# A convolution stage of eight image pairs: the work between two pairs is placed inside the steps of the next pair

## The reference, cut to what matters

```
x = x + L0(groupnorm(x))      # L0: minus the L1 distance between 3x3 patches and 128 filters
                              #     -sum over channel, tap of |W - patch|
out = act_quant(bn(conv3x3(x, wq1)))          # wq1, wq2: 4-bit weights, 7 of 9 taps kept
x = act_quant(bn(conv3x3(out, wq2)) + x)      # clip to 0..1, round to 15 levels
# then two layers on 784 tokens per image: additive attention, mixture of experts,
# linear attention, spectral filter; the change doesn't touch them
```

## Time and profile before

| | |
|---|---|
| median of 3 runs | 13612.95 us (13599.4 to 13621.69) |
| the profiled execution | 13581.18 us, span 13579.4 us |
| mean granted TensorE clock | 0.977 of full speed |
| PE busy | 12646.4 us, 93% |
| DVE busy | 11715.2 us, 86% |
| ACT busy | 11095.8 us, 82% |

### The profile page before, as it was taken

One profiled execution on the slowest core, in us unless ns is written; L12 is line 12 of the kernel. 1 busy time (PEld: TensorE's weight loads), 2 busy tenths in 40 slices (PEclk: granted clock), 3 DMA queues, 4 the chain that ended last, 5 costly groups with the idle time before them and its releaser, 6 DMA issues. The chain is left out here.

```text
span 13579.4 us, 320458 instructions
## 1 busy us (share of the span) xinstructions
PE 12646.4 (93%) x128658; PEld 6147.6 (45%) x128658; DVE 11715.2 (86%) x21048; ACT 11095.8 (82%) x7140; POOL 254.3 (2%) x125
## 2 busy tenths in 40 slices
PE   8999999999999999999867999999999999999999
PEld 3433433333333333333323455555555555555556
DVE  8888888888988888888799988998888998888981
ACT  7878778787887878878688888888888888888882
POOL 0000000000000000000000000000000000000000
PEclk9999999999999999999989999999999999999999
DMA  0000000000000000000010111111111111111113
GB/s 11 2 6 2 4 4 2 6 2 6 2 2 6 2 6 2 2 6 2 14 48 2 40 48 50 48 51 44 46 47 50 49 49 46 45 49 50 46 51 104
DMA packets 290098, 356.95 MB, mean 26 GB/s; under 512 B 28040, under 2 KB 242960, under 8 KB 288656
## 3 DMA queue, kind: packets, MB, share of 16 engines
q1 hardware_dynamic: 288656, 335.48, 8.4%
HBM read 314.14 MB, written 21.23 MB: 25 GB/s over the span
## 5 line engine op out<-in xcount | busy, mean ns | idle before, releaser
L139 PE MATMUL c_acc<-c_ring,c_onehot 128*32 128x392 f32 x73728 | 6128.9, 495 | 235.3 <-DVE c_ring L260 145.0
L260 DVE TENSOR_SCALAR c_ring<-c_xn,c_w 128x1568 f32 x5760 | 5642.3, 1048 | 648.9 <-PE c_acc L139 642.8
L186 ACT ACTIVATE c_ring<-c_xn,c_w_neg 128x1568 f32 x3456 | 5331.2, 1606 | 980.5 <-PE c_acc L139 962.6
L887 ACT ACTIVATE t_ring<-t_ring 128x3136 f32<-128x3136 f32 (+4 forms) x2160 | 5138.8, 2403 | 552.2 <-DVE t_ring L1189 536.5
L1189 DVE TENSOR_SCALAR t_ring<-t_proj 128x784 f32<-128x784 f32 (+4 forms) x10240 | 4276.1, 489 | 564.3 <-PE t_psS L798 551.0
L139 PEld LDWEIGHTS c_acc<-c_ring,c_onehot 128*32 128x32 f32 x73728 | 2472.5, 111 | 3891.7 <-issue 3746.9
L798 PE MATMUL t_psS<-t_ring,t_vhot 128*32 128x392 f32 (+3 forms) x36864 | 2834.0, 436 | 189.4 <-ACT t_ring L887 159.1
L755 PE MATMUL t_psC<-t_filter_work 128*128 128x392 f32 (+3 forms) x6144 | 1645.3, 402 | 47.5 <-ACT t_filter_work L874 47.5
L798 PEld LDWEIGHTS t_psS<-t_ring,t_vhot 128*32 128x32 f32 x36864 | 1027.1, 111 | 1248.5 <-issue 555.4
L755 PEld LDWEIGHTS t_psC<-t_filter_work 128*128 128x128 f32 x6144 | 1135.2, 192 | 710.3 <-ACT t_filter_work L874 65.6
L766 PE MATMUL t_psS<-t_filter_work 128*128 128x98 f32 (+2 forms) x4096 | 956.2, 356 | 0.0
(11 more groups left out here) (212 smaller groups left out, 3375.6 us busy)
## 6 DMA issues: line engine op xcount, KB each, us to landing
t_filter_work<-in_toep_dram SPq DMA_DIRECT2D x256, 393.0 KB, 3.3
t_filter_work<-mix_scratch SPq DMA_DIRECT2D x512, 192.0 KB, 2.4
t_filter_work<-in_toep_dram SPq DMA_DIRECT2D x256, 197.0 KB, 2.6
t_filter_work<-mix_scratch SPq DMA_DIRECT2D x512, 64.0 KB, 1.8
mix_scratch<-t_filter_work SPq DMA_DIRECT2D x4, 2048.0 KB, 9.5
c_xin<-in_x_dram SPq DMA_DIRECT2D x8, 784.0 KB, 4.3
x_scratch<-c_xout SPq DMA_DIRECT2D x8, 784.0 KB, 3.4
t_proj<-x_scratch SPq DMA_DIRECT2D x16, 392.0 KB, 3.2
```

What stands on the lines that cost most here:

```text
L139: mm = pe.matmul(acc[32 * g:32 * g + 32, ch, 0:HALF], onehot[:, 31 - r:63 - r], ring[:, r % RING, g, ch * HALF:(ch + 1) * HALF], start=Fal ...
L186: act.activation(ring[:, r % RING, g, :].rearrange("c (i h w) -> c i h w", i=2, h=HW), xn[:, :, bass.ds(dy, HW), bass.ds(dx, HW)], ACT.Rel ...
L260: dve.tensor_scalar(ring[:, r % RING, g, :].rearrange("c (i h w) -> c i h w", i=2, h=HW), xn[:, :, bass.ds(dy, HW), bass.ds(dx, HW)], w0[: ...
L887: act.activation(ring[:, st % RINGS, 0:n], ring[:, st % RINGS, 0:n], ACT.Tanh).then_inc(th.s, 1)
```

## The change: what it does

- The loops over the taps are gone. All 288 steps are written out, in one body per pair; pairs 0 and 7 have a body of their own, and pairs 1 to 6 run as three turns of a loop over two bodies (`pairs`). xin and xn get two buffers, used in turn; x1 gets a tensor of its own (x1p), and the convolutions write to three PSUM banks of their own (pst).
- Each engine walks through the steps of pair p and, after fixed step numbers, issues pieces of other work (`tracks`): the x1 of pair p-1 (after step 2), its convolutions (steps 7 to 41), the norm of pair p+1 (steps 60 to 112), the pair's own box sums (steps 130 to 150).
- The box sums move from POOL to DVE. Their PE part is inside the steps. The zero matmuls that opened acc go; step 0 opens it with start=True. Two operations per pair are new on DVE: xin less the weights' sum (s_xs). x1 is then one operation per bank that reads acc, where it was three for all.
- Which engine makes a tile is set by a running sum of costs (`distance_steps`), in which EXTRA_VEC stands for DVE's other work. MERGED is 0, so the "merged" form never occurs and every tap keeps a tile.
- At step 0 PE waits, bank by bank, until DVE has read acc. The token stage is as before.

```diff
-VEC_SHARE = [3 if r % 2 == 0 else 2 for r in range(32)]
-VEC_TILES = sum(VEC_SHARE); ACT_TILES = 4 * 32 - VEC_TILES
+MERGED = 0; TAP_A, TAP_B = 0, 1
...
+COST = dict(vec=0.95, act=1.55, merge=1.85)
...
+    out = []
...
+    for s in range(steps):
+        if s in EXTRA_VEC: vec += EXTRA_VEC[s]
...
+                e = "vec" if vec + COST["vec"] <= act + COST["act"] else "act"
+                if e == "vec": vec += COST["vec"]
+                else: act += COST["act"]
...
+        out.append(step)
...
+AT_X1 = 2
+AT_C1 = [7, 11, 15, 19]
+AT_A1 = [c + 6 for c in AT_C1]
+AT_Q = [c + 8 for c in AT_C1]
+AT_C2 = [22, 24, 30, 32]
+AT_OUT = [c + 5 for c in AT_C2]
...
+AT_GN = dict(stats=60, aggr=65, mean=72, dev=78, devs=86, var=92, std=96, xn=104, shift=110)
...
+AT_BOX = [130, 134, 138, 142]; AT_BOX_SUM = 150
+EXTRA_VEC = {AT_X1: 2.6, **{s: 0.8 for s in AT_Q}, **{s + 2: 2.2 for s in AT_OUT}, 62: 2.5, 66: 0.5, 80: 0.6, 93: 0.5, 106: 1.4, 111: 1.1, **{s: 1.9 for s in AT_BOX}}
+DISTANCE = distance_steps()
...
+            one_pair(0, 0, True, False)
+            with e.Fori(0, (NP - 2) // 2) as pp:
+                one_pair(2 * pp + 1, 1, False, False, pp)
+                one_pair(2 * pp + 2, 0, False, False, pp)
+            one_pair(NP - 1, 1, False, True)
...
+        def in_step(step, due, tracks):
+            for n, track in enumerate(tracks):
+                while due[n] is not None and due[n] <= step:
+                    due[n] = next(track, None)
+        def run(tracks, body):
+            due = [next(track, None) for track in tracks]
+            body(lambda step: in_step(step, due, tracks))
+            in_step(999, due, tracks)
...
+                sp.dma_start(x1[bass.ds(p, 1)].rearrange("a i c t -> c (a i) t"), tmp[:, :, :].rearrange("c (i h) t -> c i (h t)", i=2)).then_inc(s_st, 16)
...
+                    wait(sp, s_x1, 4 * p)
+                    wait(sp, s_x, 16 * p + 16)
+                    sp.dma_start(xin2[:, 1 - buf], ai["x"][bass.ds(p + 1, 1)].rearrange("a i c t -> c (a i) t")).then_inc(s_x, 16)
+                if not first: store(p - 1)
...
-            with pool.Fori(0, NP) as p:
-                pool.wait_ge(s_xn, 2 * p + 2)
...
-                link(pool.tensor_tensor(rows3[:, :, :, :], xn[:, :, :, 0:HW], xn[:, :, :, 1:1 + HW], ALU.add), 1)
-                link(pool.tensor_tensor(rows3[:, :, :, :], rows3[:, :, :, :], xn[:, :, :, 2:2 + HW], ALU.add), 2)
...
-                link(pool.tensor_tensor(box[:, :, :, :], rows3[:, :, 0:HW, :], rows3[:, :, 1:1 + HW, :], ALU.add), 3)
-                pool.tensor_tensor(box[:, :, :, :], box[:, :, :, :], rows3[:, :, 2:2 + HW, :], ALU.add).then_inc(s_box, 1)
...
+            def normalize(q):
+                yield AT_GN["mean"]
+                wait(pe, s_stat, 2 * q + 2)
                 pe.matmul(psg[:, 0:4], group_avg[:, :], mv[:, :, :], start=True, stop=True).then_inc(s_gmean, 1)
-                pe.wait_ge(s_dev, p + 1)
+                yield AT_GN["devs"]
+                wait(pe, s_dev, q + 1)
                 pe.matmul(psg[:, 8:10], group_avg[:, :], dev2[:, :], start=True, stop=True).then_inc(s_gdev, 1)
...
+            def tail(d):
+                for c in range(4):
+                    yield AT_C1[c]
+                    if c == 0:
+                        wait(pe, s_x1, 4 * d + 4)
+                        wait(pe, s_accr, 4 * d)
+                    if c == 3: wait(pe, s_a1, 4 * d + 1)
+                    conv(pst[:, c % 3, 0:HALF], wq1, x1p, c // 2, c % 2, s_c1)
+                for c in range(4):
+                    yield AT_C2[c]
+                    if c % 2 == 0: wait(pe, s_q, 4 * d + c + 2)
+                    if c < 3: wait(pe, s_a1, 4 * d + c + 2)
+                    else: wait(pe, s_accr, 4 * d + 1)
+                    conv(pst[:, (c + 1) % 3, 0:HALF], wq2b, xq, c // 2, c % 2, s_c2)
+            def box_sum(p):
+                yield AT_BOX_SUM
+                wait(pe, s_box, p + 1)
...
+                    pe.matmul(acc[:, ch, 0:HALF], minus_half[:, :], box[:, ch // 2, ROWS * (ch % 2):ROWS * (ch % 2 + 1), :].rearrange("c h w -> c (h w)"), start=False, stop=False, skip_group_check=True)
...
-                    pe.matmul(acc[:, ch, 0:HALF], zero_bf[:, 0:128], zero_bf[:, 128:128 + HALF], start=True, stop=False, skip_group_check=True)
...
+                def body(done):
+                    for s, step in enumerate(DISTANCE):
+                        wait(pe, s_tv, VEC_UP[-1] * p + VEC_UP[s])
+                        wait(pe, s_ta, ACT_UP[-1] * p + ACT_UP[s])
+                        for ch in range(4):
+                            if s == 0 and not first: wait(pe, s_x1, 4 * (p - 1) + ch + 1)
+                            for g in range(4):
+                                r = step[g][2]
+                                mm = pe.matmul(acc[32 * g:32 * g + 32, ch, 0:HALF], onehot[:, 31 - r:63 - r], ring[:, s % RING, g, ch * HALF:(ch + 1) * HALF],
+                                               start=(s == 0), stop=(s == NSTEP - 1), skip_group_check=True)
+                            if s == NSTEP - 1 and ch < 3: mm.then_inc(s_acc, 1)
+                        mm.then_inc(s_free, 1)
...
+                yield AT_GN["std"]
+                wait(act, s_gvar, q + 1)
                 act.activation(gstd[:, :], gvar[:, :], ACT.Sqrt).then_inc(s_gstd, 1)
...
+            def tail(d):
                 for c in range(4):
...
+                    yield AT_A1[c]
+                    wait(act, s_c1, 4 * d + c + 1)
+                    act.activation(act1[:, c, :], pst[:, c % 3, 0:HALF], ACT.Relu, scale=bn_q[:, 0:1], bias=bn_shift[:, 0:1]).then_inc(s_a1, 1)
...
-                    dve.tensor_scalar(xn[:, im, 1:1 + HW, 1:1 + HW], xin[:, im, :].rearrange("c (h w) -> c h w", h=HW), gmv[:, im, 0:1], grstd[:, im:im + 1], ALU.subtract, ALU.mult).then_inc(s_xn, 1)
-                dve.wait_ge(s_xn, 2 * p + 2)
-                n[0] += 1; dve.memset(pad[:, 0:1], 0.0).then_inc(s_v, 1)
-                with dve.Fori(0, 3) as dy:
-                    with dve.Fori(0, 3) as dx:
...
-                        for r in range(32):
...
-                link(dve.tensor_scalar(tmp[:, :, :], acc[:, :, 0:HALF], -2.0, w0_sum[:, 0:1], ALU.mult, ALU.subtract))
...
+                    yield AT_GN["shift"] + 2 * im
+                    wait(dve, s_xn, 2 * q + 2)
+                    dve.tensor_scalar(xin[:, im, :], xin[:, im, :], w0_sum[:, 0:1], None, ALU.subtract).then_inc(s_xs, 1)
+            def box_sums(p, buf):
...
+                k.do(dve.tensor_tensor(rows3[:, :, :, :], xn[:, :, :, 0:HW], xn[:, :, :, 1:1 + HW], ALU.add))
+                yield AT_BOX[1]
+                k.sync()
+                k.do(dve.tensor_tensor(rows3[:, :, :, :], rows3[:, :, :, :], xn[:, :, :, 2:2 + HW], ALU.add))
...
+                k.do(dve.tensor_tensor(box[:, :, :, :], rows3[:, :, 0:HW, :], rows3[:, :, 1:1 + HW, :], ALU.add))
...
+                dve.tensor_tensor(box[:, :, :, :], box[:, :, :, :], rows3[:, :, 2:2 + HW, :], ALU.add).then_inc(s_box, 1)
+            def distance_read(d, buf):
+                yield AT_X1
...
+                    else: wait(dve, s_free, NSTEP * (d + 1))
+                    dve.scalar_tensor_tensor(out=rows(x1p, im, h), in0=plane(acc[:, c, 0:HALF]), scalar=-2.0, in1=plane(xin2[:, buf, im, h * HALF:(h + 1) * HALF]), op0=ALU.mult, op1=ALU.add).then_inc(s_x1, 1)
+            def quant(d, c):
+                im, h = c // 2, c % 2
+                yield AT_Q[c]
+                wait(dve, s_a1, 4 * d + c + 1)
+                k.do(dve.tensor_scalar(act1[:, c, :], act1[:, c, :], 1.0, LEVELS, ALU.min, ALU.mult))
...
+                yield AT_Q[c] + 1
...
+                dve.tensor_scalar(rows(xq, im, h), plane(act1[:, c, :]), ROUND, ROUND, ALU.add, ALU.subtract).then_inc(s_q, 1)
...
+                yield AT_OUT[c]
...
+                dve.scalar_tensor_tensor(out=plane(tmp[:, c, :]), in0=plane(pst[:, (c + 1) % 3, 0:HALF]), scalar=bn_q[:, 1:2], in1=rows(x1p, im, h), op0=ALU.mult, op1=ALU.add).then_inc(s_accr, 1)
+                yield AT_OUT[c] + 1
...
+                k.do(dve.tensor_scalar(tmp[:, c, :], tmp[:, c, :], bn_shift[:, 1:2], 0.0, ALU.add, ALU.max))
...
+                dve.tensor_scalar(tmp[:, c, :], tmp[:, c, :], 1.0 / LEVELS, None, ALU.mult).then_inc(s_o, 1)
...
+                tracks = [box_sums(p, buf)]
+                if not first: tracks = [distance_read(p - 1, 1 - buf)] + tracks + tail(p - 1)
+                if not last: tracks.append(normalize(p + 1, 1 - buf))
...
+                    for s, step in enumerate(DISTANCE):
+                        wait(dve, s_free, NSTEP * p + s + 1 - RING)
```

More of the change, by code:

```diff
@@ L69, in _, with store @@
                 sp.dma_start(bn[:, n:n + 1], ai[k].rearrange("(c o) -> c o", o=1)).then_inc(s_ld, 16)
[L70 to L74, removed]
+            def store(p):
                 sp.wait_ge(s_o, 4 * p + 4)
-                sp.dma_start(x1[bass.ds(p, 1)].rearrange("a i c t -> c (a i) t"), xout[:, :, :]).then_inc(s_st, 16)
```

(35 more changed lines are left out.)

308 lines of the change are left out of this document (159 added, 149 removed).

## The result

The changed kernel takes 13185.3 us (median of 4 runs, 13184.5 to 13187.9), the kernel before 13606.2 us (median of 4, 13589.0 to 13621.7): ratio 0.969, 95% interval 0.968 to 0.971, 421 us less. The forecast was 13285 us, and its range of 13220 to 13400 us missed the result by 35 us. By the profiled executions the gain is smaller: spans of 13579.4 and 13186.1 us, 393 us less; the execution of before that was profiled took 13581.2 us, less than any of the four.

A forecast was written before the change was run, and what follows sets the result against it. PE was taken as the bound within a convolution-stage tap. Terms -129.7 (taps), -180.6 (gaps), -21.6 (clock), -7 (start), -1.4 (end), +12.3 (pair-loop turns) sum to -328 us: 13612.95 becomes 13285 us, range 13220 to 13400.

The forecast's parts named there:

- the clock within the taps: Taps of 86.17 us instead of 84.47 were momentary clock dips; 5 us a pair kept for dips, no gain counted.
- the late start (c): Last 13.2 us of the gap between pairs: 8.6 us of PE waiting after step 0's tiles were thought done.
- the gap's other parts: Between pairs: seven gaps shrink from 57.5 to 31.7 us (-180.6); the clock after them gives -21.6; pair-loop turns cost +12.3.
- the first start: Start of pair 0: the 8.6 us wait goes, less 1.1 us for two shifts of xin; -7 us.
- The loops over taps: PE's 64 turns from tap to tap, 2.03 us each, vanish when steps are written out: -129.7 us.
- The turns of the loop over pairs: The new loop over two pairs turns back twice, at the token stage's 6.11 us idle each: +12.3 us.
- The handover at step 0: PE waits at a pair's first step until DVE has read acc: 1.2 us, range 0.6 to 8.3.
- a pair's other work: PE's convolutions, box, norm matmuls and switches in each pair, 30.5 us; with the step 0 wait, 31.7 us.
- Cover on DVE and ACT: Extra work hides under PE's stream: 90 us to spare on DVE, 100 on ACT per pair, so no cost.
- handover wait: Rival: at pair ends DVE isn't ahead and PE waits up to 8.3 us; 50 us lost, 13335 us, chance 0.12.
- starved ring: Rival: DVE or ACT bounds steps 7 to 41, the tile ring runs dry; 164 us lost, 13449 us, chance 0.09.
- the slower rival: PE works nearly without pause and the granted clock falls; at 0.90 the kernel takes 13920 us; chance 0.04.

The follow-up runs named there:

- the bare kernel with box sums on DVE: Kernel before with tap loops written out and the four box sums moved from POOL to DVE, work between pairs not overlapped: 13360.2 us, ratio 0.983.

## Why the prediction missed

The direction and the bound were right, the sum was 65 us short by the traces (328 against 393) and 93 us by the medians. The steps that failed are two: the sum gave nothing for the clock within the taps, whose dips went (26 us of the 65), and it laid the late start (c) to the loops, where it was POOL's box sums. The rest are terms of a wrong size. By spans, the taps gave 28 us more than forecast, the gap's other parts 40 more, and (c) with the first start 3 less.

- **The loops over taps.** -129.7 us predicted; the experiment that does only this has a span of 13421.3 us, 158 less. The turns were a little undersized: the idle time leaves out 0.16 us of each (2.19 x 64 = 140). Against them stand gaps that are 2.2 us longer there (1629.6 to 1688.7, against 56.9 in the earlier trace rows), 15 us in seven, by DVE's turn. **The term that failed is the clock's.** I read the taps of 86.17 us as dips that would stay ("the clock had dipped for a moment"): I kept 5 us a pair for them in the new kernel's 797 and nothing for their going in the sum. They go with the pauses: 15 rows of taps were 1.7 us longer, 26 us in the profiled execution. 140 - 15 + 26 = 151 us, against 152.8 in the stage. The kernel before also scatters: its runs lie between 13572 and 13622 us over the four groups of runs, the four of the changed kernel within 3.4 us. The gain by medians is 28 us above that by traces, and more dips in a usual run than in the profiled one would explain it; that is inferred from the scatter, not measured.
- **(c), the late start of a pair.** 8.6 us in each of eight was about the right amount (69 us, where the experiment has 64), laid to entering the loops. It was POOL's box sums: the prediction took 0.964 us for tiles of 3.0 to 4.3 us. That the total hardly suffered is luck. I took off 8.6 us with the loops and priced the move to DVE at nothing; by experiment the move is worth 64 us, and with no loop left to enter the start was as late as before. With the sums left on POOL this term would have been some 66 us too good, and would have hidden the others: that kernel's span is 327.5 us under the one of before, just my 328.
- **The gap's other parts.** By my sum without (c) and the start, -131 us; the traces of the bare kernel with box sums on DVE and of the changed one differ by 171 us, 40 more. Three terms make 43 us. The turns of the loop over pairs cost 1.67 and 1.95 us, not 6.1: the token stage's row was the wrong neighbour, and a tap's turn, which I had as the low end, the right one (9 us). The handover at step 0 costs nothing outside those two turns, and a pair's other work takes 29.1 us (788.0 less 288 steps of 2.635), not 31.7 (18 us). And the bare kernel's gap is 51.2 us (798.24 to 849.39), 2.3 us more than the earlier trace rows less (c), so there was more to win (16 us). This last term and the 15 us under the taps are the same turn of DVE, which neither the kernel before nor the changed one has to pay. Without it the 65 us are dips 26, a pair's other work 18, breaks 10 and turns 9, which make 63.
- **The first start** was right in size: 40.01 us against 46.38, 6.4 for 7. It is (c)'s gain again, with (c)'s wrong reason.
- **Cover on DVE and ACT** was right: 703 and 449 tiles, DVE 5613 us busy of 6327 (89%), ACT 5521 (87%). The box sums cost 1.90 and 1.79 us each, 7.4 us a pair for my 8.1, and were covered.
- **The rivals.** No handover wait, no starved ring, and a clock that rose where the slower rival had it fall. None of them had the side that came true, more gain than forecast; the low end was made of small terms and of the level of the profiled execution, but not of the dips.

## What to carry to other kernels

When a stall has a size that you can't build up from rows, don't give it to the nearest suspect: divide the merged row beside it by its count first; 1.20 us for a tile of 0.964 would have shown POOL at work. Before a little work is given to an idle GpSimd, look at what it runs beside: 15 us of sums cost 8 us of PE's time per pair there, and nothing that shows on a busier VectorE. Pauses of 2 us in a TensorE-bound loop cost more than their length, and may make the time scatter; but kernels without such pauses spread over 2 to 13 us here themselves, so a spread is a hint and no proof. When a loop's body is written out, look at what its outer loop's turn costs on the other engines too.

## What the runs showed of the hardware

- Fp32 tensor_scalar tiles of 1568 columns on VectorE take 1.03 us, and 3.0 to 4.3 us beside tensor_tensor operations of GpSimd of 3.0 to 4.2 us; a ring of four steps (10.5 us of PE's work) doesn't cover 15 us of it.
- A turn of a loop costs PE 1.6 to 2.7 us over a body of 32 steps (2.0 in the mean), 1.7 to 2.2 over 96 and 1.7 to 2.0 over 576. DVE's turn of the loop over pairs went from 0.1 to 2.75 us of idle time when the loops inside its body were written out. Whether entering a loop costs PE anything is not shown: where it enters one it waits 13.2 us for DVE, which would cover it. In the token stage the pause at the turn is 6.1 us, and why it is longer stays open.
- With pauses of 1.8 us on average in PE's stream some taps of 84.47 us had a granted clock of 0.98 and took 1.7 us longer, all of them behind pauses of 1.95 us or more; 64 such pauses cost 21 us beside their own length, and 64 of 0.33 us cost 2 us.
- The same token stage took 6838 to 6844 us in the three kernels whose convolution stage had no loop over pairs, and 6828 to 6834 us in the ten others. Why stays open.
